# Identity products on TensorE at the ends of three stages of an eight-block kernel

## The chip, the cores and the metric

One Trainium2 chip, of which the kernel uses one core. A core has a matrix engine (PE), three elementwise engines (DVE, ACT, POOL), and queues that start transfers. The metric is the device time of one execution in microseconds, lower is better; the figure given for a kernel is the median of its runs.

## The reference

The model has four layers, each a gated attention and a gated feed-forward block, over x of shape (4, 1024, 256) with a context of 77 rows per batch:

```python
x = x + tanh(g_xattn[0]) * L0_xattn(layernorm(x), ctx, mask)   # 16 heads of 16
x = x + tanh(g_ffn[0])   * L0_ffn(layernorm(x))                # 32 low-rank experts, top 2
x = x + tanh(g_xattn[1]) * L1_xattn(layernorm(x), ctx)         # 16 heads of 64
x = x + tanh(g_ffn[1])   * L1_ffn(layernorm(x))                # ternary weights, 8-bit activations
x = x + tanh(g_xattn[2]) * L2_xattn(layernorm(x), ctx)         # causal self-attention, then context attention
x = x + tanh(g_ffn[2])   * L2_ffn(layernorm(x))                # 8 routed experts
x = x + tanh(g_xattn[3]) * L3_xattn(layernorm(x), ctx)         # one head of 256
x = x + tanh(g_ffn[3])   * L3_ffn(layernorm(x))                # 8 experts, top 2
```

Layer 1's attention, which the first part of the change touches, is `softmax(q k^T * 64**-0.5) v`, then `relu(out @ w_out1) @ w_out2` and a layer norm with gamma. The ternary block rounds weights to -1, 0, 1 and activations to 8 bits, computes `silu(x @ gate) * (x @ up)` (1024 wide), rounds again and multiplies by `down`. Layer 2's attention runs a causal self-attention with a residual norm `a`, a context attention with queries from `a`, `c = layernorm(c + c)`, `f = relu(c @ Wf + bf)` and `layernorm(c + f)`. The identity products of the change compute nothing of this.

## The kernel before, in words

x stays on the chip (`x_sb`, 128 partitions x 32 tiles of 256). The program is a row of stages, each a block in which every engine has its own instruction list, in the order of the code; no scheduler changes it. At the end of a block each engine drains and reports; when the last one has, POOL releases them all. Then `clear_semaphores` (L4567) is a short block of its own, with a second such meeting. We call the stretch from the last work of one stage to the first of the next a seam. A stage's PE list often ends some microseconds before its DVE or POOL list, since the last norm and the residual addition are theirs.

Three seams matter here.

- Seam 1, from `fold_stage` (layer 1's attention, L172) to `ternary_stage` (L2393). PE's last work is `combine` (L366). DVE then does `stats2`, `scale2` and `finish2` (L571), which adds into x. The ternary stage begins with DVE's `quantise(0)` (L2552); PE turns the tile (`turn_x`, L2457), ACT copies it (L2495), PE multiplies by gate and up (`widen`, L2467), ACT takes silu (L2502), DVE multiplies (L2557). PE's order there is `steps((widen, 3), (turn_h, 5), (narrow, 6), (turn_x, 1))`: two tiles are turned before the first is widened. DVE's list also holds the norms of the tiles ahead (L2531 to L2546).
- Seam 2, from the ternary stage to `self_stage` (L3269). PE's last work is `narrow` (L2484); DVE's is the norm of the next stage's first eight tiles (L2579). The self stage begins with POOL's constants (L4120 to L4124), on which PE waits; then PE turns the eight tiles (L3657, 16 transposes), ACT copies them out (L3848), PE projects q and k (L3667), ACT and DVE split each result in three bf16 parts (L3848, L3987 to L3991), and SyncE and POOL write the parts to memory (L3554, L4163) and read them back in another layout before the first scores (L3639).
- Seam 3, from `cross_stage` (layer 2's context attention, L1247) to `front_stage` (L2635, layer 2's experts and layer 3's attention). PE's last work is `forward` (L1485), DVE's the last addition into x (L1841). The front stage begins on PE with the folding of layer 3's weights (L2770, L2777, L2783, L2786), on DVE with the norms of two groups (L3110, L3056), on POOL with the normalising of the first group (L3248), which PE turns at L2875.

Other places in the kernel have identity products already: ten at L4354, 31 at L2880, 18 at L4517.

Of the kernel before, what the change touches and what calls it, by code (L numbers as in the profile page):

```python
# [6 lines left out]
P = 128  # L7
# [164 lines left out]
def fold_stage(chip, dram):  # L172

    nc, w = chip.nc, chip.w
# [6 lines left out]
    with ExitStack() as ctx:  # L181
# [6 lines left out]
        S_ps = [ctx.enter_context(nc.psum_tensor(f"L1_scores{i}", [P, 2, 512], F32)) for i in range(2)]  # L188
# [47 lines left out]
        def rows(c):  # L236
            return P if c < KCH - 1 else KLAST
# [39 lines left out]
        def _(pe):  # L277
# [44 lines left out]
            def turn_x(g):  # L322
                pe.wait_ge(xn_done, CH * (g + 1))
                for k in range(KD):
                    o = bank(FILL["x", g, k])
                    for i in range(CH):
                        mm = nc.tensor.transpose(o[:, i * P:(i + 1) * P], xn[:, i, k * P:(k + 1) * P], chip.ident[:])
                    mm.then_inc(ring_full, 1)

            def scores(U):  # L330
                g, u = divmod(U, UN)
                i, hf = u // 2, u % 2
                if u == 0:
                    pe.wait_ge(ring_free, emptied("x", g, KD - 1))
                pe.wait_ge(shifted, U + 1)
                for a in range(2):
                    for k in range(KD):
                        mm = nc.tensor.matmul(S_ps[U % 2][:, a, 0:BK], xT[:, g % 2, k, i * P:(i + 1) * P],  # L338
                                              kfold[:, batch_of(g), k, hf * HK + a * BK:hf * HK + (a + 1) * BK], start=(k == 0), stop=(k == KD - 1))
                mm.then_inc(s_full, 1)  # L340

            def turn(U):
                pe.wait_ge(p_done, U + 1)
                pe.wait_ge(t_free, U + 1)
                for c in range(KCH):
                    mm = nc.tensor.transpose(T_ps[0:rows(c), c * P:(c + 1) * P], prob[:, U % PBUF, c * P:c * P + rows(c)], chip.ident[:])
                mm.then_inc(t_full, 1)
# [38 lines left out]
            for s in range(UNITS + UN + 2):  # L386
                g, u = divmod(s, UN)
                if s < UNITS:
                    scores(s)
                if u == 0 and g + 1 < G:  # L390
                    turn_x(g + 1)
                if g >= 2 and u < 2:
                    combine(g - 2, 2 * u)
                    combine(g - 2, 2 * u + 1)
                if s == SUM_AT:
                    sum_weights()
                if 1 <= g <= G and u >= 2:
                    gather(g - 1, (u - 2) // 3, (u - 2) % 3)
                if 0 <= s - LAG < UNITS:
                    turn(s - LAG)  # L400

        def take(eng, copy, which):

# [843 lines left out]
def cross_stage(chip, dram):  # L1247

    nc, w = chip.nc, chip.w
# [6 lines left out]
    with ExitStack() as ctx:  # L1256
# [6 lines left out]
        S_ps = ctx.enter_context(nc.psum_tensor("L2_scores", [P, ROW_GROUPS, 512], F32))  # L1263
# [105 lines left out]
        def _(pe):  # L1369
# [16 lines left out]
            def values(b):  # L1386
                o = bank("v", b)[:].rearrange("p (f n) -> p f n", f=2)
                pe.wait_ge(rep_done, KD)
                wv = [w["L2_Wv"][:, k, :].rearrange("p (f n) -> p f n", f=2) for k in range(KD)]
                for ch in range(KCH):  # L1390
                    start = ch * P % NC
                    for k in range(KD):
                        mm = nc.tensor.matmul(o[:, :, AT[ch]:AT[ch] + WIDTH[ch]], crep[:, k, b, start:start + P],
                                              wv[k][:, :, HEAD[ch] * 16:HEAD[ch] * 16 + WIDTH[ch]], start=(k == 0), stop=(k == KD - 1))
                mm.then_inc(ring_full, 1)
# [130 lines left out]
            for g in range(1, SPAN):  # L1526
                now, ahead, old, older, oldest = g < G, g + 1 < G, 1 <= g <= G, 2 <= g <= G + 1, 3 <= g <= G + 2
                if oldest:
                    forward(g - 3, 0)
                if old:  # L1530
                    turn(UN * (g - 1) + 4)
                if g == 1:
                    turn(5)
                if now:
                    scores(UN * g)
                if g == 1:
                    values(0)
                if ahead:
                    turn_x(g + 1, 0)
                if oldest:  # L1540
                    forward(g - 3, 1)
                if 1 < g <= G:
                    turn(UN * (g - 1) + 5)
                if oldest:
                    forward(g - 3, 2)
                if ahead:
                    turn_x(g + 1, 1)
                if old:
                    turn(UN * (g - 1) + 6)
                if now:  # L1550
                    scores(UN * g + 2)
                if oldest:
                    forward(g - 3, 3)
                if old:
                    turn(UN * (g - 1) + 7)
                    gather(g - 1, 0)
                    gather(g - 1, 1)
                if older:
                    turn_n(g - 2, 0)
                if now:  # L1560
                    turn(UN * g)
                    scores(UN * g + 4)
                if older:
                    turn_n(g - 2, 1)
                if old:
                    combine(g - 1, 0)
                if now:
                    turn(UN * g + 1)
                if ahead:
                    query(g + 1, 0)  # L1570
                if now:
                    scores(UN * g + 6)
                    turn(UN * g + 2)
                if old:
                    combine(g - 1, 1)
                if ahead:
                    query(g + 1, 1)
                if now:
                    turn(UN * g + 3)
                if g % 2 and (g + 1) // 2 < B:  # L1580
                    values((g + 1) // 2)

        @block.scalar
        def _(act):
# [808 lines left out]
def ternary_stage(chip, dram, norm):  # L2393


    nc, w = chip.nc, chip.w
# [11 lines left out]
    with ExitStack() as ctx:  # L2408
# [6 lines left out]
        g_ps, u_ps = ps("gate_ps", [P, INNER]), ps("up_ps", [P, INNER])  # L2415
# [23 lines left out]
        def steps(*phases):  # L2439
            for at in range(1, LAST):  # L2440
                for phase, behind in phases:
                    if 0 <= at - behind < T:
                        phase(at - behind)
# [6 lines left out]
        @block.tensor  # L2450
        def _(pe):
            def turn_x(t):
                pe.wait_ge(s["xq_done"], t + 1)
                if t:
                    pe.wait_ge(s["xT_free"], t)
                for k in range(KD):
                    mm = nc.tensor.transpose(xT_ps[:, k * P:(k + 1) * P], xq[:, t % 2, k * P:(k + 1) * P], chip.ident[:])  # L2457
                mm.then_inc(s["xT_full"], 1)

            def widen(t):  # L2460
                pe.wait_ge(s["xT_free"], t + 1)
                for o, n, full, free in ((g_ps, "gate", "g_full", "silu_done"), (u_ps, "up", "u_full", "h_done")):
                    if t:
                        pe.wait_ge(s[free], t)
                    for c in range(INNER // 512):
                        for k in range(KD):
                            mm = nc.tensor.matmul(o[:, c * 512:(c + 1) * 512], xT[:, t % 4, k, :], tern[n][:, k, c * 512:(c + 1) * 512],  # L2467
                                                  start=(k == 0), stop=(k == KD - 1))
                    mm.then_inc(s[full], 1)

            def turn_h(t):
                pe.wait_ge(s["hq_done"], t + 1)
                if t:
                    pe.wait_ge(s["hT_free"], t)
                for k in range(IK):
                    mm = nc.tensor.transpose(hT_ps[:, k * P:(k + 1) * P], hq[:, t % 2, k * P:(k + 1) * P], chip.ident[:])
                mm.then_inc(s["hT_full"], 1)

            def narrow(t):
                pe.wait_ge(s["hT_free"], t + 1)  # L2480
                if t:
                    pe.wait_ge(s["o_free"], t)
                for k in range(IK):
                    mm = nc.tensor.matmul(o_ps[:, 0:D], hT[:, t % 2, k, :], tern["down"][k], start=(k == 0), stop=(k == IK - 1))  # L2484
                mm.then_inc(s["o_full"], 1)

            steps((widen, 3), (turn_h, 5), (narrow, 6), (turn_x, 1))

        @block.scalar
        def _(act):  # L2490
# [2252 lines left out]
```

## Time and profile before

| | us |
|---|---|
| median of 3 runs | 2559.74 (2557.93 to 2561.8) |
| the profiled execution | 2555.28 |
| its span | 2553.5 |
| PE busy | 2328.7 (91%) |
| DVE busy | 1717.2 (67%) |
| ACT busy | 1242.8 (49%) |
| POOL busy | 1299.3 (51%) |

The profile is one execution. The span runs from its first to its last instruction; 1.8 us of the execution lie outside it. Busy PE is time in which a matmul is in flight. The granted clock (PEclk) is TensorE's clock as a share of full speed, 1.00 for 2.4 GHz and 0.50 for 1.2 GHz. In a timeline row the bracket gives the idle time of the engine before the row, and what ended it. A plain f32 product is two rows of the trace (x2), an f32 transpose one.

### The profile page before, as it was taken

Reading aid. Unit: us, or ns where it says so; the run is one execution under the profiler, and the core shown is the slowest. Engines: PE = TensorE matmul, PEld = TensorE weight load, DVE = VectorE, ACT = ScalarE, POOL = GpSimd, SP = SyncE. Lnnn points to the kernel's source line nnn. Section 1 sums busy time; section 2 is a strip of 40 time slices with the busy share of each in tenths; the row PEclk is TensorE's granted clock in tenths of the full one; section 3 lists DMA queues with packets and bytes.
Section 4 is the critical chain, followed back from the end, with each engine's and each line's share of the span. In section 5 each row is a group of like instructions: output and inputs, shape, how many; then the busy total and the mean of one; then the engine's idle time right before and its main releaser. Section 6 shows DMA issues by size and latency. Waiting matters only on the chain. (4 is left out here: it accounts for less than half of the span.)

```text
span 2553.5 us, 46249 instructions
## 1 busy us (share of the span) xinstructions
PE 2328.7 (91%) x14740; PEld 1563.7 (61%) x14741; DVE 1717.2 (67%) x3560; ACT 1242.8 (49%) x2483; POOL 1299.3 (51%) x2079
## 2 busy tenths in 40 slices
PE   6997998999997997999999999889969985999998
PEld 4664886666664663445444454356646664999998
DVE  5995774655557976777868778489976656444443
ACT  4773544444442882666666666557753430111111
POOL 3675772234444653333443535467875313666664
PEclk9998999999998998999999999999989987999999
DMA  4001000000100005131231221110005150322232
GB/s 147 6 1 71 0 0 1 1 1 1 50 1 17 1 1 139 32 94 36 66 87 39 70 73 39 34 42 18 9 1 174 50 209 20 49 49 47 48 47 36
DMA packets 86135, 115.44 MB, mean 45 GB/s; under 512 B 15480, under 2 KB 65536, under 8 KB 84272
## 3 DMA queue, kind: packets, MB, share of 16 engines
q1 hardware_dynamic: 67408, 92.65, 12.1%
q0 software_dynamic: 18528, 20.31, 4.9%
q8 instruction: 104, 1.70, 0.3%
q14 instruction: 95, 0.78, 0.1%
HBM read 78.01 MB, written 34.64 MB: 44 GB/s over the span
## 5 line engine op out<-in xcount | busy, mean ns | idle before, releaser
L3893 ACT ACTIVATE L2S_pT<-L2S_t_ps 128x512 f32<-128x512 f32 (+3 forms) x768 | 356.5, 491 | 220.8 <-PE L2S_t_ps L3717 212.0
L3957 DVE TENSOR_REDUCE L2S_mx<-L2S_s_ps 128x1 f32<-128x768 f32 (+7 forms) x384 | 350.0, 950 | 104.2 <-PE L2S_s_ps L3640 103.6
L3717 PE MATMUL L2S_t_ps<-L2S_q,L2S_k 98*128 98x512 bf16 (+3 forms) x768 | 249.2, 335 | 17.7 <-DMA L2S_q<-L2S_mrow 7.2
L4191 POOL TENSOR_SCALAR_AFFINE_SELECT L2S_pT<-L2S_pT 128x128 f32<-128x128 f32 x512 | 152.3, 312 | 174.0 <-ACT L2S_pT L3893 169.6
L3639 PE MATMUL L2S_s_ps<-L2S_k,L2S_q 96*128 96x512 bf16 (+3 forms) x768 | 199.0, 331 | 11.9 <-DVE L2S_mx L3957 8.1
L702 POOL TENSOR_TENSOR L_prob<-L_prob,L_rc 128x616 f32<-128x616 f32 x64 | 82.3, 1287 | 231.3 <-DVE L_rc L607 231.3
L3717 PEld LDWEIGHTS L2S_t_ps<-L2S_q,L2S_k 98*128 98x128 bf16 x768 | 72.9, 97 | 196.4 <-ACT L2S_pT L3893 127.6
L3817 PE MATMUL L2S_o_ps<-L2S_pT,L2S_v 128*32 128x512 f32 (+3 forms) x1536 | 165.4, 504 | 0.0
L4529 ACT ACTIVATE L3B_xT<-L3B_xT_ps 128x256 f32<-128x256 f32 x71 | 27.3, 384 | 260.9 <-PE L3B_xT_ps L4493 251.5
L338 PE MATMUL L_scores<-weights,L_xT 128*128 128x308 f32 x512 | 143.1, 423 | 2.3 <-ACT L_xT L461 1.6
L4467 POOL DMA_INDIRECT L3B_xb<-expert_rows,L3F_rows x71 | 80.2, 1129 | 126.9 <-PE L3B_xT_ps L4493 68.2
L4557 DVE TENSOR_TENSOR L3B_h<-L3B_si,L3B_u_ps 128x512 f32<-128x512 f32 x71 | 48.8, 687 | 137.3 <-issue 108.8
L4503 PE MATMUL L3B_u_ps<-L3B_xT,weights 128*128 128x128 f32 x1136 | 139.0, 275 | 1.3 <-issue 1.3
L4503 PE MATMUL L3B_g_ps<-L3B_xT,weights 128*128 128x128 f32 x1136 | 140.1, 277 | 0.0
L4477 POOL DMA_INDIRECT out<-L3B_y,L3F_rows x71 | 115.1, 1620 | 44.7 <-issue 21.0
L606 DVE TENSOR_REDUCE L_sm<-L_prob 128x8 f32<-128x616 f32 x64 | 50.8, 794 | 129.3 <-ACT L_prob L465 129.1
L4513 PE MATMUL L3B_o_ps<-L3F_wo,L3B_h 128*128 x568 | 134.5, 380 | 1.3 <-issue 1.3
L4503 PEld LDWEIGHTS L3B_g_ps<-L3B_xT,weights 128*128 128x128 f32 x1136 | 134.1, 194 | 0.1
L4503 PEld LDWEIGHTS L3B_u_ps<-L3B_xT,weights 128*128 128x128 f32 x1136 | 132.9, 192 | 1.7 <-issue 1.7
L4141 POOL DMA_DIRECT2D L2S_q<-L2S_mrow x64 | 32.8, 515 | 185.4 <-DVE L2S_mrow L3963 185.2
L1196 POOL TENSOR_TENSOR L_prob<-L_prob,L_rc 128x616 f32<-128x616 f32 x64 | 77.2, 1220 | 67.1 <-DVE L_rc L1126 66.9
L338 PEld LDWEIGHTS L_scores<-weights,L_xT 128*128 128x128 f32 x512 | 92.4, 190 | 29.5 <-issue 1.9
(571 smaller groups left out, 5886.4 us busy)
## 6 DMA issues: line engine op xcount, KB each, us to landing
qk_parts<-L2S_part SPq DMA_DIRECT2D x84, 128.0 KB, 2.4
L2S_q<-qk_parts SPq DMA_DIRECT2D x32, 192.0 KB, 3.4
L2S_k<-qk_parts SPq DMA_DIRECT2D x30, 192.0 KB, 3.4
L2S_q<-qk_parts SPq DMA_DIRECT2D x32, 128.0 KB, 3.2
L3F_w<-in_L_gu SPq DMA_DIRECT2D x8, 512.0 KB, 7.4
weights<-in_L_w SPq DMA_DIRECT2D x8, 512.0 KB, 9.6
out<-x_sb SPq DMA_DIRECT2D x8, 512.0 KB, 3.3
expert_rows<-L3F_xn SPq DMA_DIRECT2D x8, 512.0 KB, 3.8
```

The source lines that it names most:

```text
L338: mm = nc.tensor.matmul(S_ps[U % 2][:, a, 0:BK], xT[:, g % 2, k, i * P:(i + 1) * P], kfold[:, batch_of(g), k, hf * HK + a * BK:hf * HK + ( ...
L702: nc.gpsimd.tensor_tensor(p, p, wide(rc[:, U % 4, :].unsqueeze(2), [P, HH, NC]), ALU.mult).then_inc(p_done, 1)
L3639: nc.tensor.matmul(o[:, z * 512 + c:z * 512 + e], lhs, k6[0:KR, q % 2, h, c:e], start=True, stop=(e < end))
L3717: nc.tensor.matmul(o[:, lo:512], k6[:, q % 2, j, kt * P:(kt + 1) * P], q6[:, q % 2, c, j, lo:512], start=True, stop=True).then_inc(s["t_fu ...
L3817: mm = nc.tensor.matmul(o_ps[32 * j:32 * j + 32, lo:512], v[:, kt, h * VC:h * VC + 32], pT[:, st % SLOTS, j, lo:512], start=(kt == 0), sto ...
L3893: nc.scalar.activation(pT[:, st % SLOTS, j, lo:512], t_ps[j % 2][:, lo:512], ACT.Exp, scale=SK).then_inc(s["exp_done"], 1)
L3957: nc.vector.tensor_reduce(dst, src, AX.X, ALU.max).then_inc(s["mx_done"], 1)
L4191: nc.gpsimd.affine_select(out=edge, in_=edge, compare_op=ALU.is_ge, fill=0.0, base=0, pattern=[[1, P]], channel_multiplier=-1).then_inc(s[ ...
L4467: nc.gpsimd.indirect_dma_start(xb[:, j % AHEAD, :], None, dram["rows"], bass.IndirectOffsetOnAxis(rows[:, 0, j:j + 1], 0)).then_inc(loaded ...
L4477: nc.gpsimd.indirect_dma_start(dram["out"], bass.IndirectOffsetOnAxis(rows[:, 1, j:j + 1], 0), y[:, j % AHEAD, :], None, compute_op=ALU.ad ...
L4503: mm = nc.tensor.matmul(o[q % 2][:, c * P:(c + 1) * P], own[:, q % 2, m, k, c * P:(c + 1) * P], xT[:, q % 2, k, :], start=(k == 0), stop=( ...
L4513: mm = nc.tensor.matmul(o_ps[q % 2][:, 0:D], h[:, q % 2, k, :], wo[:, k, bass.ds(e * D, D)], start=(k == 0), stop=(k == FK - 1))
```

## The change

After its last real work in each of the three stages PE multiplies the 128x128 f32 identity by itself, 21, 7 and 36 times, into a PSUM bank that the stage no longer reads. Nothing waits for a result, and the products wait for nothing. Nothing is removed.

```diff
@@ fold_stage, end of PE's list @@
+            for _ in range(21):
+                nc.tensor.matmul(S_ps[0][:, 0, 0:P], chip.ident[:], chip.ident[:], start=True, stop=True)
@@ cross_stage, end of PE's list @@
+            for _ in range(36):
+                nc.tensor.matmul(S_ps[:, 0, 0:P], chip.ident[:], chip.ident[:], start=True, stop=True)
@@ ternary_stage, end of PE's list @@
             steps((widen, 3), (turn_h, 5), (narrow, 6), (turn_x, 1))
+            for _ in range(7):
+                nc.tensor.matmul(g_ps[:, 0:P], chip.ident[:], chip.ident[:], start=True, stop=True)
```

PE's instruction list at seam 1, before. The two branches are the end of the block and of the one that clears semaphores.

```order
L356 MATMUL L_ring<-L_probT,weights 128x512 x17
L366 MATMUL L_ring<-weights,L_oT 128x256 x8
L181 UNCONDITIONAL_BRANCH
L2450 UNCONDITIONAL_BRANCH
L2457 MATMUL L1F_xT_ps<-ident,L1F_xq 128x128 x4
L2467 MATMUL L1F_gate_ps<-weights,L1F_xT 128x512 x4
```

And after; lines below the edit have moved by 2 and 4.

```order
L356 MATMUL L_ring<-L_probT,weights 128x512 x17
L366 MATMUL L_ring<-weights,L_oT 128x256 x8
L402 MATMUL L_scores<-ident 128x128 x21
L181 UNCONDITIONAL_BRANCH
L2454 UNCONDITIONAL_BRANCH
L2461 MATMUL L1F_xT_ps<-ident,L1F_xq 128x128 x4
L2471 MATMUL L1F_gate_ps<-weights,L1F_xT 128x512 x4
```

The 21 products (L402) stand behind `combine` and ahead of the end of the block.

PE's list at seam 2, before: `turn_h` and `narrow` of the last tiles, then the self stage's transposes.

```order
L2476 MATMUL L1F_hT_ps<-ident,L1F_hq 128x128 x8
L2484 MATMUL L1F_o_ps<-weights,L1F_hT 128x256 x16
L2408 UNCONDITIONAL_BRANCH
L3622 UNCONDITIONAL_BRANCH
L3657 MATMUL L2S_s_ps<-ident,L2S_xn 128x128 x16
L3667 MATMUL L2S_s_ps<-L2S_xT,weights 128x512 x8
```

And after:

```order
L2480 MATMUL L1F_hT_ps<-ident,L1F_hq 128x128 x8
L2488 MATMUL L1F_o_ps<-weights,L1F_hT 128x256 x16
L2493 MATMUL L1F_gate_ps<-ident 128x128 x7
L2412 UNCONDITIONAL_BRANCH
L3628 UNCONDITIONAL_BRANCH
L3663 MATMUL L2S_s_ps<-ident,L2S_xn 128x128 x16
L3673 MATMUL L2S_s_ps<-L2S_xT,weights 128x512 x8
```

The seven products (L2493) follow the last `narrow`; the transposes come next, behind the two meetings.

PE's list at seam 3, before: the last `forward`, then the folding of layer 3's weights.

```order
L1483 MATMUL L_ring<-L_brow,L_ones_b 128x256
L1485 MATMUL L_ring<-weights 128x256 x2
L1256 UNCONDITIONAL_BRANCH
L2764 UNCONDITIONAL_BRANCH
L2770 MATMUL L_o_ps<-ctxT_sb,weights 128x308 x4
L2777 MATMUL L_turn_ps<-weights,ctxT_sb 77x256 x8
```

And after:

```order
L1485 MATMUL L_ring<-L_brow,L_ones_b 128x256
L1487 MATMUL L_ring<-weights 128x256 x2
L1585 MATMUL L_scores<-ident 128x128 x36
L1258 UNCONDITIONAL_BRANCH
L2770 UNCONDITIONAL_BRANCH
L2776 MATMUL L_o_ps<-ctxT_sb,weights 128x308 x4
L2783 MATMUL L_turn_ps<-weights,ctxT_sb 77x256 x8
```

The 36 products (L1585) follow `forward`. The lists of the other engines are unchanged.

## Rows read from the trace of the kernel before

**Rows 1.** Engines and granted clock by stretch (from:to, length, busy per engine).

```profile
core 0: us, PE busy (x) PEld busy (x) DVE busy (x) ACT busy (x) POOL busy (x), PEclk, DMA share, GB/s
1000.00:1638.00 638.00, 606.02 (x4117) 273.25 (x4118) 471.70 (x750) 399.38 (x865) 254.01 (x642) 0.98 0.22 58
784.20:789.00 4.80, 4.80 (x15) 2.45 (x16) 4.58 (x12) 0.70 (x1) 2.19 (x2) 1.00 0.00 0
813.00:819.80 6.80, 5.09 (x15) 2.40 (x16) 6.28 (x26) 3.04 (x5) 1.67 (x4) 0.50 0.47 154
949.60:952.90 3.30, 3.30 (x17) 2.48 (x16) 2.52 (x14) 2.30 (x3) 1.89 (x6) 0.50 0.00 0
959.80:966.50 6.70, 5.95 (x19) 4.48 (x20) 1.97 (x1) 2.39 (x4) 6.26 (x2) 0.50 0.86 288
1895.10:1901.80 6.70, 5.54 (x18) 4.30 (x19) 5.44 (x14) 3.08 (x6) 6.13 (x10) 0.50 0.01 2
1908.70:1918.90 10.20, 4.80 (x10) 3.16 (x11) 7.54 (x28) 2.62 (x6) 2.62 (x4) 0.50 0.14 27
```

**Rows 2.** Timeline of PE: start, length; the 18 identity products already there.

```profile
2140.03 4.26 PE L4517 MATMUL L3B_xT_ps<-ident 128*128 128x128 f32 x36 [1.18 <-PEq L4569]
```

**Rows 3.** Timeline of all engines at seam 1.

```profile
802.83 3.72 PE L366 MATMUL L_ring<-weights,L_oT 128*128 128x256 f32 x16 [0.69 <-ACT L_oT L475]
...
810.12 1.67 DVE L571 SCALAR_TENSOR_TENSOR x_sb<-L_res,L_rs,x_sb 128x256 f32<-128x256 f32 x4
...
813.43 0.69 PE L2457 MATMUL L1F_xT_ps<-ident,L1F_xq 128*128 128x128 f32 x2 [6.88 <-DVE L1F_xq L2552]
...
817.83 1.11 ACT L2502 ACTIVATE L1F_h<-L1F_gate_ps,weights 128x1024 f32<-128x1024 f32 x1 [1.32 <-PE L1F_gate_ps L2467]
...
821.08 1.21 DVE L2557 TENSOR_TENSOR L1F_h<-L1F_h,L1F_up_ps 128x1024 f32<-128x1024 f32 x1
```

**Rows 4.** All waits of DVE, 813 to 903 us: total, times, longest.

```profile
DVE L1F_xq L2552 <- POOLq L2617: 1.2, 1, 1.2
DVE L1F_xn L2541 <- POOL L1F_rs L2594: 1.1, 2, 0.7
```

**Rows 5.** Timeline of all engines at seam 2.

```profile
954.31 3.89 DVE L2579 TENSOR_SCALAR L2S_xn<-x_sb,L2S_mv,L2S_rs 128x256 f32<-128x256 f32 x8 [2.16 <-POOL L2S_rs L2631]
...
955.36 1.03 PE L2484 MATMUL L1F_o_ps<-weights,L1F_hT 128*128 128x256 bf16 x8 [0.70 <-ACT L1F_res L2520]
...
960.55 3.65 PE L3657 MATMUL L2S_s_ps<-ident,L2S_xn 128*128 128x128 f32 x16 [4.15 <-POOL L2S_cmask L4124]
961.67 0.60 ACT L3848 ACTIVATE L2S_xT<-L2S_s_ps 128x512 f32<-128x512 f32 x1 [4.76 <-PE L2S_s_ps L3657]
...
967.20 0.60 ACT L3848 ACTIVATE L2S_part<-L2S_s_ps 128x512 bf16<-128x512 f32 x1 [2.37 <-PE L2S_s_ps L3667]
967.57 0.48 POOL L4151 TENSOR_SCALAR L2S_shift<-vecs,gates 128x256 f32<-128x256 f32 x1
967.83 0.69 DVE L3987 TENSOR_TENSOR weights<-L2S_s_ps,L2S_part 128x512 f32<-128x512 f32 x1 [5.41 <-ACT L2S_part L3848]
...
972.21 1.91 POOL L4163 DMA_DIRECT2D qk_parts<-L2S_part  x3 [4.16 <-DVE L2S_part L3991]
```

**Rows 6.** Timeline of all engines at seam 3.

```profile
1903.25 0.81 PE L1485 MATMUL L_ring<-weights 128*128 128x256 f32 x3
...
1912.36 0.42 DVE L1841 TENSOR_TENSOR x_sb<-x_sb,weights 128x256 f32<-128x256 f32 x1
...
1914.10 4.44 PE L2770 MATMUL L_o_ps<-ctxT_sb,weights 128*128 128x308 f32 x8 [10.04 <-PEq L4569]
...
1923.60 4.86 POOL L3248 TENSOR_SCALAR L3F_xn<-x_sb,L_mv,L_rs 128x256 f32<-128x256 f32 x4 [0.22 <-POOL L_rs L3236]
...
1928.52 1.09 PE L2875 MATMUL L_turn_ps<-ident,L3F_xn 128*128 128x128 f32 x8 [1.11 <-POOL L3F_xn L3248]
```

**Rows 7.** Timeline of PE: two idle times of two to three microseconds.

```profile
784.18 2.38 PE L356 MATMUL L_ring<-L_probT,weights 128*128 128x512 f32 x5 [2.75 <-ACT L_probT L471]
...
949.23 1.69 PE L2476 MATMUL L1F_hT_ps<-ident,L1F_hq 128*128 128x128 f32 x8 [2.11 <-ACT L1F_hT L2514]
```

## The prediction

> **What bounds the kernel now.** I read the page first: PE is busy for 91% of the span, so its clock is worth asking after. The view of engines and clock by stretch then shows where it was low beside the three seams: 0.50, the 1.2 GHz level, at 813.0 to 819.8, 959.8 to 966.5 and 1908.7 to 1918.9 us, each behind a long idle time of PE [rows 1]. PE worked there for 5.09, 5.95 and 4.80 us. At 1.00, the 2.4 GHz level, it would need about half, so the full clock could give back at most 2.5 + 3.0 + 2.4 = 7.9 us of PE time. The timelines of all engines decide how much of that is on the path.
>
> **The cost of the products.** The kernel's 18 identity products took 4.26 us at the full clock [rows 2], 0.237 us each. So 21 take 5.0 us, 7 take 1.7 and 36 take 8.5. PE's last rows end at 806.55 [rows 3], 956.39 [rows 5] and 1904.06 us [rows 6], and the products start about 0.2 us before these ends, for the rows overlap. They end near 811.4, 957.9 and 1912.4 us. The last DVE rows of the same blocks end at 811.79, 958.20 and 1912.78 [rows 3, 5, 6]. The meeting of the engines waits for DVE, so the products cost nothing, with 0.3 to 0.4 us to spare. If one of them ran over, everything behind the meeting would start that much later. Behind the products on PE stand only the meetings, and nobody waits for their results. Bounds on this term: 0, and in the low case each product 0.47 us (taken up as a rival).
>
> What they buy is a shorter idle time: 6.88 becomes 2.0 us, 4.15 becomes 2.6, 10.04 becomes 1.7.
>
> **Seam 1, worth 0.** If the clock stays up, PE's first work in the ternary stage is done earlier: ACT's first silu, 817.83 to 818.94 us, could come about a microsecond sooner. But DVE multiplies it only at 821.08 [rows 3], 2.1 us after it is there, since its own list (norms of the tiles ahead) is not done sooner. In all of 813 to 903 us DVE waits only 1.2 us for the stage's start and 1.1 us for POOL's power, never for PE or ACT [rows 4], and it was busy 6.28 of the 6.8 us in which the clock was low [rows 1]. DVE sets the pace. PE's saving becomes PE's waiting. Bounds: 0 and 2.5 us, half of PE's 5.09; I take 0, for no row shows DVE waiting for what would come sooner.
>
> **Seam 2, worth 2.8 us where the clock stays up.** PE starts at 960.55 us. Nobody else has work on the path until PE is done: ACT waits 4.76 us for the first turned tile and 2.37 us for the first projection, DVE waits 5.41 us [rows 5]. At the full clock 8 transposes take 1.09 us [rows 6], so the 16 end about 2.0 us after the start, at 962.5, when ACT has the first two copies out (the first 0.6 us after the start in place of 1.12, each 0.60 long). The first projection is four rows; five such rows of 512 took 2.38 us [rows 7], 0.43 apart, so four take 1.95. ACT gets it at about 964.45 in place of 967.20 us: 2.8 us sooner. Next late would be DVE and then the transfers. POOL is free from 968.05 and waits until 972.21 us for DVE [rows 5], so it can follow by the full 2.8. The splits are written to memory and read back behind this, with nothing timed by anything but this chain, and then PE is busy for 606 of 638 us [rows 1]; what is gained at its start stays gained. Bounds: 0 and 3.0 us, half of 5.95. I take 2.8.
>
> Does the clock stay up over 2.6 us of idle PE? The nearest rows disagree. After 2.75 us of idling, work at 784.2 to 789.0 us ran at 1.00; after 2.11 us the clock fell, and 949.6 to 952.9 us ran at 0.50 [rows 1, 7]. What the engine did before differs: the seven products make PE's last microseconds dense, and behind the seam it is dense as well. I give a little under one half that it stays up. An execution that keeps it gains 2.8 us, one that does not gains nothing.
>
> One rule speaks against it. The seam's first work is transposes: 16 of them, 3.65 us at the low clock, and the clock was back at full only after 966.5 us, when products had run too [rows 1, 5]. The Trainium skill, page "TensorE: Matmul & The Clock Gate", section "Part 4: PE-mode transpose", says that the full clock doesn't engage for transposes. No row here separates the two kinds. By the rule the transposes could not hold what the products kept, the clock would drop under the projections, and at most the transposes' own saving of about 1.8 us would be left: 2557.9, inside the second case below.
>
> **Seam 3, worth 0.** The folding of the weights (L2770 on) would be up to 2.4 us shorter. But PE then waits at L2875 for POOL's normalised tiles: POOL works on them from 1923.60 to 1928.46 us, and PE, early already, waited 1.11 us [rows 6]. POOL hangs on DVE's norms, and these on the start of the stage; neither waits for PE. The 2.4 us become a wait of some 3.5. Bounds: 0 and 2.4; I take 0.
>
> **The sum.** The profiled execution: 2555.28 - 2.8 = 2552.5 us. It lay 4.46 us below the median of the runs; against that, 2559.74 - 2.8 = 2556.9 us.
>
> **The rivals.**
>
> A, the forecast: the clock stays up at seam 2 in most executions, 2556.9 us.
>
> B, it falls all the same, after 2.6 us as it did after 2.11 [rows 7]. Then the products change nothing: 2559.7 us. That the change doesn't do what it says is this case too. Against it: the 2.75 us that it outlasted.
>
> C, all three pay: seams 1 and 3 have something on PE's path that the waits don't show. 2.5 + 2.8 + 2.4 = 7.7 us, 2552.0 us. For it: the clock was low at each for 6.8 to 10.2 us. Against it: DVE's 2.1 us of lateness at seam 1 and PE's 1.11 us of waiting at seam 3.
>
> D, slower: the products at seam 3 run at the low clock, and PE comes last to the meeting. In the profile the clock was 0.50 at 1895.1 to 1901.8 us [rows 1], and up only 2.3 us before the products would begin; where it comes up later, the first of them cost 0.47 in place of 0.24 us. With 18 of 36 low that is 4.3 us more, less the 0.4 to spare: 3.9 us, with no gain at seam 2, so 2563.6 us. It decides from the second low product on (0.24 each against 0.4 us). Against it: dense work had brought the clock back before the end of the stage.
>
> **How the numbers follow.** A 0.43, B 0.32, C 0.13, D 0.12. The predicted time is A's. What a measurement of this kernel can tell from no change is about 0.2%, 5.1 us. A, B and D lie inside; C lies outside on the fast side. With a little from A's and B's scatter (three runs of one kernel spread over 3.9 us): faster 0.15, same 0.80, slower 0.05. The range runs from between C and A to between B and D, 2553.5 to 2562.5 us; it leaves out about 0.2.
>
> **What would show it.** The new PE groups: 21, 7 and 36 products, 0.24 us each at clock 1.00, ended before DVE's last rows at the seams, and the meetings no later. Seam 1: DVE's first multiplication still about 8.1 us after the stage's first row, with silu waiting longer for it. Seam 2: the granted clock 1.00 from the first transpose on (case A), 16 transposes in 2.0 in place of 3.65 us, ACT's first split at 3.9 in place of 6.65 us after PE's start. Seam 3: L2875's counterpart waits about 3.5 us for POOL. The prediction is wrong if DVE at seam 1 or POOL at seam 3 starts its work sooner relative to the stage's first row, if PE reports last at a meeting, or if the 2.8 us of seam 2 are lost behind the read of q and k before 1000 us.

## The result, and the profile after

| | before | after |
|---|---|---|
| median of 20 runs each | 2559.98 us | 2564.91 us |
| the profiled execution | 2555.28 us | 2570.47 us |

The ratio after to before is 1.0025, with an interval from 1.0017 to 1.0032: 6.4 us slower by the ratio, 4.9 us by the two medians. The forecast was 2556.9 us. The profiled execution is the slowest of its 20 runs, 5.6 us over their median, so it holds more loss than a usual run.

Engines and granted clock by stretch, in the profile after:

```profile
core 0: us, PE busy (x), PEclk, DMA share, GB/s
816.50:823.30 6.80, 5.95 (x16) 0.50 0.38 142
963.20:966.60 3.40, 3.40 (x16) 0.51 0.78 223
1936.00:1946.20 10.20, 10.20 (x25) 0.50 1.06 401
```

Behind seam 1 the clock was low for as long as before [rows 1]. Behind seam 2 it was low for 3.4 us in place of 6.8. Behind seam 3 the folding of the weights ran at full clock, but a low stretch of 10.2 us follows later, with PE busy for all of it.

Seam 1, from the timelines of PE, ACT and DVE:

```profile
815.39 0.44 PE L2461 MATMUL L1F_xT_ps<-ident,L1F_xq 128*128 128x128 f32 x2 [2.19 <-DVE L1F_xq L2558]
...
819.79 1.11 ACT L2508 ACTIVATE L1F_h<-L1F_gate_ps,weights 128x1024 f32<-128x1024 f32 x1 [1.32 <-PE L1F_gate_ps L2471]
...
823.04 1.21 DVE L2563 TENSOR_TENSOR L1F_h<-L1F_h,L1F_up_ps 128x1024 f32<-128x1024 f32 x1
```

PE idles for 2.19 in place of 6.88 us. ACT's silu comes 4.40 us after PE's first row, DVE's first multiplication 7.65 us after it, both as before [rows 3].

Seam 2, from the timelines of PE and ACT:

```profile
958.18 1.73 PE L2493 MATMUL L1F_gate_ps<-ident 128*128 128x128 f32 x14
962.82 3.25 PE L3663 MATMUL L2S_s_ps<-ident,L2S_xn 128*128 128x128 f32 x16 [2.92 <-POOL L2S_cmask L4130]
...
968.19 0.60 ACT L3854 ACTIVATE L2S_part<-L2S_s_ps 128x512 bf16<-128x512 f32 x1 [1.48 <-PE L2S_s_ps L3673]
```

ACT's first split comes 5.37 us after PE's start; it was 6.65 [rows 5], and 3.9 was forecast for a clock that stays up. Here it fell 0.4 us after PE's start (second stretch above).

Seam 3, timeline of PE:

```profile
1910.53 8.20 PE L1585 MATMUL L_scores<-ident 128*128 128x128 f32 x72
1920.72 2.31 PE L2776 MATMUL L_o_ps<-ctxT_sb,weights 128*128 128x308 f32 x8 [2.00 <-PEq L4575]
...
1931.08 0.60 PE L2816 MATMUL L_turn_ps<-ident,L_wrow 128*8 128x128 f32 x4 [0.34 <-ACT weights L2985]
1934.97 1.09 PE L2881 MATMUL L_turn_ps<-ident,L3F_xn 128*128 128x128 f32 x8 [3.29 <-POOL L3F_xn L3254]
1935.99 3.75 PE L2827 MATMUL L_o_ps<-L3F_xn 8*128 8x256 f32 x8
...
1942.48 3.70 PE L2849 MATMUL L_o_ps<-weights,L3F_w 128*128 128x512 f32 x4
```

The products ran at the full clock and ended at 1918.73 us; DVE's last row of the block ended at 1919.40. The folding of the weights starts with 2.31 in place of 4.44 us, and PE then waits 3.29 us for POOL in place of 1.11 [rows 6]. Both are what the prediction said. But the rows behind the wait are PE's own pace: the experts' bias products (8 rows of the array, L2827, in `routed_bias`) took 3.75 us.

One loss stands at no seam. Layer 2's self-attention runs its two middle batches in a loop (`Fori(1, B - 1)`; the expectations below call it the context attention by mistake). Where it jumps back for the second of them, PE idled once in the kernel before (first fence) and twice after (second):

```profile
1331.12 0.39 PE L3717 MATMUL L2S_t_ps<-L2S_q,L2S_k 98*128 98x512 bf16 x1 [2.00 <-issue]
```

```profile
1334.23 0.39 PE L3723 MATMUL L2S_t_ps<-L2S_q,L2S_k 98*128 98x512 bf16 x1 [1.77 <-issue]
...
1337.62 0.29 PE L3645 MATMUL L2S_s_ps<-L2S_k,L2S_q 96*128 96x128 bf16 x1 [2.42 <-issue]
```

"issue" means that no semaphore and no other engine that the trace shows was waited for. At the starts of the batches that need no jump back (1168 and 1495 us before) PE does not idle.

To find where time goes, take the same DVE instruction in two traces and subtract its starts: the shift. What the shift grows by in a stretch is lost there. Against the kernel before:

| kernel | 1321 to 1345 us | 1914 to 1945 us | 2075 to 2200 us |
|---|---|---|---|
| the change | 2.9 | 3.1 | 5.7 |
| 21 products alone | 0.0 | -0.1 | 0.6 |
| 7 alone | 0.0 | 0.0 | 0.9 |
| 36 alone | -1.4 | 5.9 | 0.7 |
| 36 alone, again | -1.6 | 5.7 | 1.4 |
| 36 and the wait filled | -1.8 | 0.1 | 0.4 |
| the same, again | -0.1 | 2.8 | 6.0 |
| the change and the wait filled | 3.2 | 2.4 | 4.3 |
| 64 one-column products | 3.0 | -0.1 | 0.7 |
| 21, 7 and 36 one-column | 3.0 | -0.1 | 1.0 |
| 4 products in the wait | -0.1 | -0.1 | 0.6 |
| 24 one-column at seam 1 | 0.4 | 0.1 | 0.6 |
| 28 one-column at seam 1 | 3.8 | 0.0 | |
| seams 1 and 2 in 10 wide products | 0.2 | -0.1 | 0.8 |
| the change in 19 wide products | 0.2 | 3.3 | |
| the change, bias products moved up | 2.8 | 0.3 | |
| before, bias products moved up | -1.8 | 3.4 | |
| 36 alone, bias products of 128 rows | -0.2 | 2.7 | |
| before, bias products of 128 rows | -0.1 | -1.8 | |

One profile each, so the small numbers are read as a pattern only. (The last column is left empty for six profiles from two other chips, in all of which that stretch ran 1.0 to 5.3 us faster.) The first column shows some 3 us lost where 28 or more instructions were added ahead of that place, and nowhere else. The second shows a loss in nearly every kernel with the 36 (not in one of two profiles with the wait filled, and hardly in the change with the bias products moved up), and in the kernel before with the bias products moved up. The third follows the second in part: at the end of the front stage the clock was low for 13.7 us after (first fence: from:to, length, PE busy, clock, DMA), and for 6.8 before (second).

```profile
2093.10:2106.80 13.70, 13.34 (x60) 0.50 1.07 392
```

```profile
2082.70:2089.50 6.80, 6.80 (x28) 0.50 1.07 398
```

### The profile page after: what moved, and what is told of

Read it like the earlier page. It is cut to its first block and busy times, and to the rows that moved or that the text cites. A ratio compares the mean times of both kernels' runs of the same rounds, so it can differ in the third digit from the quotient of the medians.

```text
span 2568.7 us, 46505 instructions
## 1 busy us (share of the span) xinstructions
PE 2356.0 (92%) x14868; PEld 1589.2 (62%) x14869; DVE 1716.7 (67%) x3560; ACT 1243.5 (48%) x2483; POOL 1300.4 (51%) x2079
## 5 line engine op out<-in xcount | busy, mean ns | idle before, releaser
L4519 PEld LDWEIGHTS L3B_o_ps<-L3F_wo,L3B_h 128*128 128x128 f32 x568 | 103.6, 192 | 13.2 <-issue 1.8
```

The costliest lines, as they stand in the source:

```text
L4519: mm = nc.tensor.matmul(o_ps[q % 2][:, 0:D], h[:, q % 2, k, :], wo[:, k, bass.ds(e * D, D)], start=(k == 0), stop=(k == FK - 1))
```

## The experiments

Theory G: the loss is made at seam 3, where PE folds sooner, waits longer for POOL, and finds the clock low behind that wait. Rival L: the longer list of instructions costs, wherever they stand. Rival Q: where the clock falls is chance that any shift of the program deals anew.

**One seam at a time.** The edit of the change, at one place only.

> Only the 21 products behind layer 1's attention. Theory G (the loss is made at seam 3: PE folds layer 3's weights sooner, then idles longer for POOL, and its clock falls in the dense work behind): 0, within 1.5 us of before. Rival L (the loss comes with the longer instruction list, a third of it here): +1.5 to +2. Rival Q (nothing but which idle times the clock happens to survive, all along the program): anything between -3 and +3, and not the parts' sum.

> Only the 7 products behind the ternary experts. Theory G: 0 to -1 us; in the profile the clock falls at seam 2 all the same or stays up. Rival L: +0.5. Rival Q: between -3 and +3 us.

> Only the 36 products behind layer 2's context attention. Theory G: the whole loss, +3 to +5 us, made between 1925 and 1950 us: a low clock of 7 to 10 us in the front stage where before it was 3.4. Rival L: +2.5 to +3, not at one place. Rival Q: between -3 and +3 us.

Measured: 21 alone 1.0005 (0.9994 to 1.0016), 7 alone 1.0005 (0.9996 to 1.0014), 36 alone 1.0038 (1.0025 to 1.0051). The clock behind the seam, and two of the rows, in the profile with the 36 alone:

```profile
1934.60:1948.30 13.70, 13.00 (x36) 0.50 1.06 398
```

```profile
1935.30 1.97 PE L2877 MATMUL L_turn_ps<-ident,L3F_xn 128*128 128x128 f32 x8 [3.18 <-POOL L3F_xn L3250]
1937.20 3.78 PE L2823 MATMUL L_o_ps<-L3F_xn 8*128 8x256 f32 x8
```

The loss comes with the products of seam 3, as G says, but is twice G's 3 to 5 us: some 9.7 us by the ratio, of which the profile places 5.9 at the seam. Seams 1 and 2 give nothing that can be told.

**The length of the list.**

```diff
-                nc.tensor.matmul(S_ps[:, 0, 0:P], chip.ident[:], chip.ident[:], start=True, stop=True)
+                nc.tensor.matmul(S_ps[0:1, 0, 0:1], chip.ident[:, 0:1], chip.ident[:, 0:1], start=True, stop=True)
```

> The same 64 matmuls at the same places with one column of the identity as each operand: the list is as long as in the changed kernel, PE's work is nearly nil. Theory G: 0, within 1.5 us of before. Rival L: the whole loss, +5 us. Rival Q: like before, for hardly any time is moved.

> The change with as many instructions, but the 36 at seam 3 are products of one column and one row, that keep PE busy for little. PE idles at seam 3 as before, the clock falls there as before, the wait for POOL is about 1.1 us. Theory G: no loss at seam 3, ratio 0.9995 to 1.001. Rival L: as the change, 1.0025, for the list is as long. Rival Q: anywhere from 0.998 to 1.004. The 64 one-column products alone came out at 1.0023 with an interval from 1.0012 to 1.0035, which speaks for L or Q; this run says whether it repeats.

Measured: all 64 of one column 1.0023 (1.0012 to 1.0035); only seam 3's 36 of one column, the 28 full, 1.0015 (1.0005 to 1.0024). G alone had said no loss, so G is not all of it. Both profiles show the second idle time with releaser issue and 3.0 us lost there, and nothing at seam 3. Two runs count the instructions (one-column products at seam 1), and two do the same work with fewer:

```diff
+            for _ in range(5):
+                nc.tensor.matmul(S_ps[0][:, 0, :].rearrange("p (o c) -> p o c", o=4), chip.ident[:], wide(chip.ident[:].rearrange("p (o c) -> p o c", o=1), [P, 4, P]), start=True, stop=True)
```

> 24 products of one column and one row at seam 1, only the trace is wanted. If the second idle time comes in a step, it is there with some 2.4 us or not there at all; if it grows with the list, it has a length between 0 and 2.4 us. At 21 it was not there, at 28 it had 2.3 to 2.8 us.

> Only 28 products of one column and one row at the end of layer 1's attention (seam 1), which take next to no time; nothing at the other seams. Theory L2: the second idle time of PE with releaser issue at 1332 to 1338 us appears, and 3 us are lost there: ratio 1.0008 to 1.0018, where the 21 full products at the same place gave 1.0005 (0.9994 to 1.0016) and no such idle time. If the number of instructions does not matter: no second idle time, ratio 0.9995 to 1.0005.

> As much product work at the three seams with fewer instructions: 5 products of 512 columns and one of 128 in place of 21, one and three in place of 7, nine in place of 36; 19 instructions in place of 64, 10 of them ahead of layer 2's context attention in place of 28. Theory L2: the second idle time with releaser issue at 1332 to 1338 us is gone, 3 us are won against the change; what is left is the loss of seam 3, ratio 1.0005 to 1.0018. If the number of instructions does not matter (rival to L2): the second idle time is there, ratio 1.0025 as the change.

> The product work of the change at seams 1 and 2 in 10 instructions (5 products of 512 columns and one of 128; one and three), nothing at seam 3. If the two causes are the second idle time with releaser issue and seam 3's longer wait: neither is there, ratio 0.9994 to 1.0006, and no idle time at 1332 to 1340 us beyond the one of 2 us. If the products at seams 1 and 2 themselves cost something: 1.001 or more, as 21 and 7 alone gave 1.0005 each. If seam 2's kept clock pays as forecast: 0.999.

The idle times with releaser issue there, with 24 (first fence; one execution only, so it has no ratio) and with 28:

```profile
1333.66 0.39 PE L3719 MATMUL L2S_t_ps<-L2S_q,L2S_k 98*128 98x512 bf16 x1 [2.30 <-issue]
```

```profile
1338.42 0.39 PE L3719 MATMUL L2S_t_ps<-L2S_q,L2S_k 98*128 98x512 bf16 x1 [2.25 <-issue]
...
1341.86 0.29 PE L3641 MATMUL L2S_s_ps<-L2S_k,L2S_q 96*128 96x128 bf16 x1 [2.47 <-issue]
```

It comes in a step, between 24 and 28 added instructions. With 28 the ratio is 1.0009 (0.9999 to 1.0018), by itself not clear of no change. With 10 wide products in place of 28 it is gone: the whole change in 19 wide products came to 1.0018 (1.0007 to 1.0028) and lost 3.3 us at seam 3, where PE again waited 3.27 us. Seams 1 and 2 in 10 wide products came to 1.0004 (0.9994 to 1.0013): nothing that can be told is lost or won. L holds, as a step at one place: six profiles have 28 or more added ahead of it and all show the second idle time, and the fourteen others don't. The Trainium skill, page "Runtime: NRT & Kernel Launch", section "Instruction fetch mechanics", says that the list is read ahead in blocks and in order, and that a jump to a place outside what is held has to read its block before it goes on. The trace agrees with the first idle time (a jump, 2.0 us). That the second is the next block, reached soon behind the jump's target once the list ahead is 28 longer, fits with the step, but no run shows the reading itself.

**Seam 3: is it the wait?** The wait is filled with products (`keep_warm(12)` ahead of the transposes of POOL's tiles), or with `routed_bias` moved ahead of them.

```diff
             routed_start()
+            keep_warm(12)
```

> The 36 products at seam 3 alone, and 12 further identity products (keep_warm) on PE between the transposes of wrow and those of the first normalised tiles, where PE waited 3.2 us for POOL with the 36 alone. They write columns that nobody reads. Theory G (the loss of seam 3 is made by PE's longer wait for POOL, during or behind which the clock falls, under work that PE itself paces): the wait shrinks to about 0.4 us, the clock is 1.00 behind it or low for one short stretch at most, and the time is 2557 to 2560 us, within 0.1% of the kernel before (ratio 0.999 to 1.001), some 8 us under the 36 alone (1.0038). Rival L (the longer list of instructions costs, wherever they stand): 48 more instructions than before, so at least as slow as the 36 alone, ratio 1.004 or more. Rival Q (where the clock falls further on is chance that any shift of the program re-deals): ratio anywhere from 0.998 to 1.004, with no difference at 1925 to 1950 us that explains it.

> The whole change (21, 7 and 36 products) and the same 12 products ahead of the first normalised tiles. Theory G: the change without its loss, ratio 0.999 to 1.001 against the kernel before, where the change had 1.0025; DVE's work behind seam 3 stands against the start of the stage as in the kernel before. Rival L: 1.003 or more, 12 instructions more than the change. Rival Q: anywhere from 0.998 to 1.004.

> The kernel before with only 4 identity products (keep_warm) between the transposes of wrow and those of the first normalised tiles, where PE waited 1.11 us for POOL. Theory G: the wait shrinks to 0.2 us and the clock, that fell for 3.4 us at 1932.6 us under the scores and the first expert products, may stay up: 0 to 1.5 us sooner, ratio 0.9992 to 1.0. Rival L: 4 instructions more, no difference to be measured, 1.0. Rival Q: anywhere from 0.998 to 1.004.

> The 36 products at seam 3 alone, a second time. Seam 3's loss made by the clock behind the longer wait: 3 to 6 us between 1914 and 1945 us of the kernel before, ratio 1.0012 to 1.0025, no second idle time at 1332 to 1340 us (none is added ahead of it). Rival: 1.0038 as the first time (five runs), and then the profile does not hold all of it.

> The 36 products and 12 more in PE's wait for POOL, a second time. If the filled wait keeps the clock in most executions: ratio 1.0 to 1.0008 and 1.0015 under the 36 alone in the same call. If the first profile was a lucky one (no loss, where its runs had 1.0026): the profile or the ratio again shows 2 to 3 us lost behind seam 3, and the wait as such is not the cause, but the clock's fall under the products of 8 rows and 1 row behind it.

Measured: 36 filled 1.0026 (1.0016 to 1.0035) and, again, 1.0027 (1.0017 to 1.0037); the change filled 1.0024 (1.0013 to 1.0035); the kernel before with 4 products in its wait 1.0003 (0.9994 to 1.0011); the 36 alone, again, 1.0033 (1.0022 to 1.0045). So G's number was wrong by 0.0026. The 36 alone came out at the rival's number again, not at the 1.0012 to 1.0025 that the 5.7 us in the profile would give: the profiles do not hold all of the loss. The first profile of the filled wait, with no loss, was the fastest of its 11 runs and misled; the second shows the loss with next to no wait:

```profile
1926.23 2.84 PE L2882 MATMUL L3F_l_ps<-ident 128*128 128x128 f32 x24
1929.67 1.09 PE L2877 MATMUL L_turn_ps<-ident,L3F_xn 128*128 128x128 f32 x8 [0.59 <-POOL L3F_xn L3251]
1930.69 1.99 PE L2823 MATMUL L_o_ps<-L3F_xn 8*128 8x256 f32 x8
...
1935.35 3.70 PE L2845 MATMUL L_o_ps<-weights,L3F_w 128*128 128x512 f32 x4
```

PE idled 0.59 us, and the clock fell all the same, right behind the products of 8 rows: the first two expert products (x4) took 3.70 us, and 1.92 at the full clock in the last run below. The wait is not the cause by itself: filling it took off 0.0012 on one chip and 0.0006 on another, both inside the noise.

The other order (`routed_bias` moved up; the number of instructions unchanged):

```diff
             routed_start()
+            routed_bias()
...
-                if i == -1:
-                    routed_bias()
```

> The change, and the experts' bias products (routed_bias, 8 rows each) moved from behind the transposes of the first normalised tiles to before them, where PE waited 3.3 us for POOL. All work is done, only PE's order differs. Theory G2 (the loss of seam 3 is made because the clock falls behind the longer wait, under the bias products and the scores that PE itself paces, 2 us of products that become 3.75): the bias products fill 2 us of the wait, behind the wait only dense work is left, and the profile shows 1945 us of the program reached 2 us or more sooner against the stage's start; ratio 1.0005 to 1.0015, since the loss made by the list's length stays. Theory L2 (a part of the change's loss has nothing to do with the seams: with 28 instructions more ahead of it, PE's list shows a second idle time of 2.3 to 2.8 us with releaser issue some 3.5 us behind the one of the kernel before in layer 2's context attention, at 1332 to 1338 us, +3 us): that idle time is there, since 28 stand ahead of it. Rival Q (only chance, at every place): the ratio is that of the change, 1.0025, give or take 0.001.

> The kernel before, with no product added and only the bias products moved ahead of the transposes of the first normalised tiles; as many instructions as before. Theory G2: they fill the 1.11 us of waiting for POOL, up to 1.1 us sooner at 1945 us against the stage's start, ratio 0.9993 to 1.0. No second idle time with releaser issue. Against: the tiles then wait for the bias products, 2.0 us of products in 1.11 us of waiting, and nothing is won.

Measured: 1.0034 (1.0022 to 1.0046) on the change, 1.0017 (1.0006 to 1.0028) on the kernel before, where 1.0005 to 1.0015 and 0.9993 to 1.0 were expected. Timeline of PE with `routed_bias` moved up in the kernel before:

```profile
1936.89 2.75 PE L2821 MATMUL L_o_ps<-L3F_xn 8*128 8x256 f32 x8 [0.68 <-ACT L3F_xn L2979]
1939.57 1.97 PE L2875 MATMUL L_turn_ps<-ident,L3F_xn 128*128 128x128 f32 x8
```

The clock fell during the 8-row products, with 0.68 us of waiting ahead of them, and 3.4 us were lost. The order made the kernel before slower; on the change 1.0034 against 1.0025 is inside the noise, although its profile lost only 0.3 us at seam 3. Next are the products themselves.

**Seam 3: the rows.** The 4 bias products are made to use all 128 rows; the routed experts' bias is left out of the computation in both.

```diff
-                        mm = nc.tensor.matmul(o[:, n * D:(n + 1) * D], wT[:, i * P:(i + 1) * P], bdn[:], start=True, stop=True)
+                        mm = nc.tensor.matmul(o[:, n * D:(n + 1) * D].rearrange("p (o c) -> p o c", o=2), chip.ident[:], wide(chip.ident[:].rearrange("p (o c) -> p o c", o=1), [P, 2, P]), start=True, stop=True)
```

> The 36 at seam 3 alone, and the experts' 4 bias products of 8 rows and 256 columns replaced by identity products of 128 rows and 256 columns (the routed experts' bias is left out of the computation, the instructions and their waits are the same in number). Theory R (few-row products behind the wait are what lets the clock fall, or keeps it low once it fell): the low stretch behind the seam is 3.4 us or gone, the products take 2 us and not 3.75, under 2 us are lost between 1914 and 1945 us against the 5.7 and 5.9 of the 36 alone, ratio 1.0 to 1.0015. If the rows do not matter and the clock falls for the idle time or by the place alone: 3 to 6 us lost, ratio 1.002 to 1.004.

> The kernel before with the same 4 products of 128 rows in place of 8 (the routed experts' bias left out of the computation). Theory R: the 3.4 us at the low clock at 1932.6 us go, 0 to 1.5 us won, ratio 0.9992 to 1.0. If the rows do not matter: the low stretch stays where it is, ratio 0.9997 to 1.0005.

Measured: with the 36, 1.0011 (1.0002 to 1.0020), where they had 1.0033 and 1.0038; in the kernel before, 0.9990 (0.9981 to 0.9999), the only kernel here that is faster than it. Stretches of both, the 36 first (PE busy, clock, DMA), then the kernel before (the busy times of all five engines stand ahead of the clock):

```profile
1930.00:1936.80 6.80, 6.23 (x18) 0.52 1.06 399
```

```profile
1930.00:1937.00 7.00, 5.97 (x33) 4.25 (x34) 1.38 (x2) 1.97 (x4) 6.85 (x21) 1.00 1.06 394
```

And the rows of the kernel before with full bias products:

```profile
1932.51 1.89 PE L2821 MATMUL L_o_ps<-ident 128*128 128x256 f32 x8
...
1935.99 1.92 PE L2843 MATMUL L_o_ps<-weights,L3F_w 128*128 128x512 f32 x4
```

Here the low stretch is gone and 1.8 us are won at seam 3. With the 36 it still comes (PE waited 3.30 us for POOL here) but for 6.8 us, where the 36 alone had 13.7. The theory had said 3.4 us or none there and under 2 us lost; 2.7 were.

What the 36 cost with full rows is the difference between these two kernels, which ran on one chip: medians of 2557.95 and 2553.41 us, 1.0011 against 0.9990, and 2.7 against -1.8 us in the table. So with full rows the 36 still cost some 0.002 of the time, 4.5 us of it at the seam; with 8 rows they cost 0.0033 and 0.0038, 5.7 and 5.9 us of it at the seam. As far as intervals of some 0.001 to either side allow, the few rows are the smaller part of the loss, and not the whole cause. Their own cost is a matter of the clock: its mean over the runs was 0.9673 with full rows and 0.9650 in the kernel before on that chip, and, with `routed_bias` moved up, 0.9634 against 0.9656 on another. Full rows and a filled wait together were not tried.

**Seam 2.** The change with the wait filled happened to keep its clock over seam 2, and is the test of the forecast. Rows from the timelines of POOL, PE, ACT and DVE (first fence), and of POOL, DVE and PE before (second):

```profile
960.84 6.92 POOL L4155 MEMSET L2S_k<- 2x8192 bf16 x1 [0.39 <-POOL L2S_cmask L4131]
960.94 1.94 PE L3664 MATMUL L2S_s_ps<-ident,L2S_xn 128*128 128x128 f32 x16 [2.74 <-POOL L2S_cmask L4131]
...
964.76 0.60 ACT L3855 ACTIVATE L2S_part<-L2S_s_ps 128x512 bf16<-128x512 f32 x1 [1.09 <-PE L2S_s_ps L3674]
...
966.12 1.93 DVE L3996 CAST L2S_part<-weights 128x512 bf16<-128x512 f32 x1
...
980.71 0.27 PE L3646 MATMUL L2S_s_ps<-L2S_k,L2S_q 96*128 96x128 bf16 x1 [3.94 <-issue]
...
981.09 2.02 PE L3682 MATMUL L2S_t_ps<-weights,L2S_xT 128*128 128x256 f32 x4
```

```profile
960.53 6.92 POOL L4148 MEMSET L2S_k<- 2x8192 bf16 x1 [0.39 <-POOL L2S_cmask L4124]
...
968.56 0.43 DVE L3989 CAST L2S_part<-weights 128x512 bf16<-128x512 f32 x1
...
981.41 0.22 PE L3639 MATMUL L2S_s_ps<-L2S_k,L2S_q 96*128 96x128 bf16 x1 [2.21 <-issue]
...
981.64 1.08 PE L3675 MATMUL L2S_t_ps<-weights,L2S_xT 128*128 128x256 f32 x4
```

The 16 transposes took 1.94 us and the first split came 3.82 us after PE's start: the forecast's 2.0 and 3.9. The clock was 1.00 under the transposes and the projections behind them, so the rival rule on transposes did not come true. The seam had begun 0.3 us later than before, and DVE's first subtraction had a shift of -2.4: 2.7 us gained.

DVE's next instruction, a cast, took 1.93 us in place of 0.43. POOL was filling `L2S_k` until 967.76 us, and the cast ended at 968.05; before, the fill was over at 967.45, and the cast began at 968.56. In all thirteen profiles in which the two overlap the cast ended 0.28 or 0.29 us after the fill, however early it began. No run moves the fill away, so that it holds the cast is read from these times alone. It left a shift of -0.9. PE was done with its projections sooner, idled 3.94 us in place of 2.21 until it could start on the scores, and had the clock low for 3.4 us from 980.4 us: its rows there took 2.02 in place of 1.08 us. The shift at 985 us was +0.8.

Three more profiles kept the clock over this seam (the change with one-column products at seam 3, the change with the bias products moved up, seams 1 and 2 in wide products). In all of them the cast took 1.97 to 2.01 us, and at 985 us DVE stood 0.5 to 0.7 us later than at the start of the seam.

## Why the prediction was wrong

**The cost of the products: right.** They ran at about 0.24 us each (1.73 us for 7, 8.20 us for 36) and ended ahead of DVE's last row. Rival D had the right sign and nearly the right time, 2563.6 us, but its mechanism didn't happen: no product at seam 3 ran at the low clock in the profile, and PE was not last to the meeting. That the measured time lies near D's is luck.

**Seam 1, worth 0: right.** In the profile after, the clock fell all the same. In five other profiles it stayed up for 3 us behind PE's first row, and ACT's silu came 3.4 to 3.6 us after PE's first row in place of 4.40, but DVE's first multiplication stood 7.64 or 7.65 us after it in every one. DVE's list gives the pace.

**Seam 2, worth 2.8 us: wrong, in the step "Next late would be DVE and then the transfers".** The chance of the clock (it stayed up in four of seven profiles with products there) and the first split were sized well. The step took DVE and POOL for engines that only wait for this chain, and its rows leave out POOL's fill, which runs until 967.45 us. Moved ahead, DVE's first cast ran beside that fill and took 1.93 to 2.01 in place of 0.43 us, more than half of the gain; the rest went in PE's low clock behind a longer idle time, 2.02 in place of 1.08 us for its first projection there. It was lost before 1000 us, which the prediction had named as a sign of being wrong. The term measured nothing that can be told: 1.0005 (0.9996 to 1.0014) for the 7 alone.

**Seam 3, worth 0: wrong, in the step "The 2.4 us become a wait of some 3.5".** The wait came, 3.29 us. The step asked whether PE's saving reaches the path, and not what clock PE's next work would have. In the kernel before, the clock is low over PE's idle time and the folding behind it, which costs nothing, for the folding is hidden; behind the wait for POOL it was low for only 3.4 us. With the 36 the clock is up for all or most of the folding, and low for 6.8 to 13.7 us around and behind the wait in all but one profile, mostly under products that PE paces. The term measured 1.0033 to 1.0038 alone, some 8.5 to 9.7 us, of which the profiles place 5.7 and 5.9 at the seam. The bias products' 8 rows and the longer wait each carry a smaller part at most; with full rows the 36 still cost some 0.002.

**A term that was missing: the list.** "Behind the products on PE stand only the meetings" counted what waits for the products, not what their place in the list moves. 28 instructions ahead of a loop brought a second idle time of 2.4 us and 2.9 us of loss in the profile; the three kernels that have it and no loss at seam 3 came to 1.0009, 1.0015 and 1.0023.

What stays open: alone, the parts come to 1.0004, 1.0009 and 1.0033 to 1.0038, together more than the change's 1.0025. They don't add, perhaps because each moves the places where the clock falls behind it; no run shows that. Nor is it shown why, with the 36 ahead, the clock is low for longer behind POOL's tiles, with few rows as with full ones: that it is low there, and what it costs, is measured, and the reason is open. The loss at the end of the front stage, 5.7 us in the profile after, was not tested apart. A product of 8 rows padded with zeros to 128, which would keep the bias and might give the 0.9990, was not tried.

## What to carry to other kernels

A clock that is kept up over one idle time may fall at the next weak spot, and it matters which work stands there: a low stretch under work that is hidden costs nothing, and is better left where it is. Products with few rows behind an idle time are worth a test with full rows. Count what an edit adds to an engine's list when a loop's jump follows, and do the same filler work in few wide products. Where a stage's start is sped up, look at what every other engine does in the time into which the work moves, before counting the gain.

## What was not expected of the hardware

- With four products of 128 rows in place of 8, the same columns and the same 2 us of a busy PE, the low stretch of 3.4 us behind them was gone in the profile, and the kernel was faster by 0.1% (0.9990, 0.9981 to 0.9999).
- The idle time behind a jump went from one of 2.0 us to two of 1.8 and 2.4 us (the change) when 28 instructions were added some 500 us ahead of it; with 24 it was still one, of 2.3 us.
- DVE's cast of 128x512 took 0.43 us alone and up to 2.01 us while POOL filled `L2S_k`: in thirteen profiles it ended 0.28 or 0.29 us after that fill.
- Sixteen f32 transposes behind 2.74 us of idle PE ran at the full clock: 1.94 us, and 3.65 at the low one.
